# Attention kernel on one core: the x bank's work and the products with v move behind the second group's pair of each step

## The chip, the cores and the metric

The kernel runs on one core of a Trainium2 chip. The metric is the device time of one execution in microseconds (us), as the median of several runs. TensorE (PE) does the matmuls, VectorE (DVE) and ScalarE (ACT) read their results, GpSimd (POOL) works in on-chip memory alone, and SyncE (SP) issues the transfers.

## What is computed

Four layers stand one behind the other, on x of shape (16, 1024, 256), each added to its input: a state-space layer, a gated feed-forward layer, causal attention, and the same feed-forward layer again. The change touches only the attention:

```
x_proj = x @ Wqkv + bqkv                 # x is the normalised input; 16 heads of 16
att = jnp.einsum('bhtd,bhsd->bhts', q, k) * (1.0 / jnp.sqrt(jnp.float32(hd)))
att = jnp.where(causal, att, jnp.float32(-jnp.inf))
att = jax.nn.softmax(att, axis=-1)
y = att @ v
return y.transpose(0, 2, 1, 3).reshape(B, T, C) @ Wproj + bproj
```

## The kernel before

The attention goes over 16 batches b, and in each over 4 quads q of four heads. A quad has 20 steps, and a step has two groups g, 0 and 1, that lie on different halves of TensorE's rows. For each step and group TensorE issues a pair: a piece of the second pass of this quad (`second_piece`, line 1657: scores of keys against queries, less the row maximum, for the exponential), and beside it a piece of the first pass of a later quad for the other group (`first_piece`, line 1633: scores whose row maxima are wanted). Steps 14 and 15 have no first pass. In what follows "pair 8.1" is that of step 8 and group 1. Where a piece touches the diagonal, two small matmuls (`masked`, line 1603) add the mask.

Each pass has three banks of PSUM that are used in turn, so a pair can only start when the reader of the pair three before it is done: `second_wait` waits for the exponential of that pair (ScalarE, line 1525, counted by `exp_done`), and `first_wait` for its maxima (VectorE, line 1427, counted by `s1_free`). Only at the start of a batch is the turn of the second pass's banks begun anew: pair 0.0 of q = 0 waits for the exponential of the pair directly before it.

Two further kinds of work stand on TensorE's queue between the pairs.

- Every odd step has a product with v (`times_v`, line 1685), of the unit of two steps whose probabilities were finished two steps ago.
- In `x_events` is written which work uses the single bank `x_ps`, and at which step: "heads" (turning the finished heads, line 1717), "turn" and "out" (the output projection of the batch before, lines 1724 and 1732), and "project" 0 to 7 for later half batches (0 and 1 transposes, line 1699; 2 to 5 parts of q and k, line 1703; 6 and 7 v, line 1709). An event at `at` is issued in step `at + 1`, so at even steps. Eight of the ten even steps have one; steps 18 and 0 have none. `x_free` hands the bank back.

The readers' queues are laid down by step: in step s ScalarE does both exponentials and then what step s has for the x bank; VectorE does the maxima of group 1's and then of group 0's first-pass piece (that is, of pair s.0 and of pair s.1), and then what step s has for the x bank (lines 1412 to 1455). Behind that, in step 6 of q = 0 and q = 2, stands the preparation of a later half batch (`prepare`, lines 1398 to 1406), which there are 15 and 14 of in the loop. The orders of VectorE, ScalarE, GpSimd and SyncE are the same in both kernels; every queue runs in its own order.

Of the kernel before, what the change touches and what calls it, by code (L numbers as in the profile page):

```python
# [991 lines left out]
def attention_phase(nc, sem, identf, identb, x2, x3, wqkv, bqkv, wproj, bproj, qk_scratch, v_scratch):  # L992
# [36 lines left out]
    def x_events(q, first, more, more2):  # L1029

        heads = [] if first and q == 0 else [(1, "heads", 0), (7 if q == 1 else 5, "heads", 1)]
        finish = [] if first else {0: [(9, "turn", 0), (11, "out", 0), (13, "turn", 1), (15, "out", 1)],
                                   1: [(3, "turn", 2), (5, "turn", 3), (9, "out", 2), (11, "out", 3)]}.get(q, [])
        project = {0: [(3, 6), (7, 7)], 1: [(13, 0), (15, 1)], 2: [(3, 2), (7, 3), (9, 4), (11, 5), (13, 6), (15, 7)],
                   3: [(3, 0), (7, 1), (9, 2), (11, 3), (13, 4), (15, 5)]}[q] if (more2 if q == 3 else more) else []
        return sorted(heads + finish + [(s, "project", j) for s, j in project])

    def flags(b):
        if isinstance(b, int):
            return b == 0, b + 1 < NB, b + 2 < NB  # L1040
        return False, True, True
# [4 lines left out]
    def x_base(b, q):  # L1046

        before = X_PROLOGUE + sum(x_count(i) for i in range(b)) if isinstance(b, int) else \
            x_count(None) * b + (X_PROLOGUE + x_count(0) - x_count(None))
        return before + sum(len(x_events(i, *flags(b))) for i in range(q))  # L1050

    def projected(b, q):

        return ((2 * b + 2, 0), (2 * b + 3, 1), (2 * b + 3, 1), (2 * b + 4, 0))[q]

    def first_pass_at(q, step, more):

        if step < UNITS1 - LEAD:
            return (1, step + LEAD) if more or q < 3 else None
        if step >= STEPS - LEAD:  # L1060
            return (2, step - (STEPS - LEAD)) if more or q < 2 else None
        return None

    with ExitStack() as ctx:
# [83 lines left out]
        with nc.Block() as block:  # L1148
# [440 lines left out]
            def _(pe):  # L1589
# [27 lines left out]
                def first_wait(quad, unit, g):  # L1617
                    if g == 1 and unit == 0:
                        for side in range(2):
                            pe.wait_ge(laid_out[side], quad + 1)  # L1620
                    use = 2 * unit + 1 - g
                    if not isinstance(quad, int) or quad > 0 or use >= 3:
                        pe.wait_ge(s1_free, 2 * UNITS1 * quad + use - 2)

                def first_piece(buf, unit, g, k):

                    p, pieces = unit // len(PASS1), PASS1[unit % len(PASS1)]
                    if k >= len(pieces):
                        return
                    bank = s1_ps[(2 * unit + 1 - g) % 3]  # L1630
                    blk, t0, t1 = pieces[k]
                    col, w = sum(HD * (u1 - u0) for _, u0, u1 in pieces[:k]), HD * (t1 - t0)
                    last = mm(bank[:, col:col + w], rows_of(qs[buf], g, KROWS, p, BT * blk, BT * (blk + 1)),  # L1633
                              rows_of(ks[buf], g, KROWS, p, t0, t1), start=k == 0,
                              stop=k == len(pieces) - 1 and not diagonals(pieces, True))
                    if k == len(pieces) - 1:
                        if diagonals(pieces, True):
                            last = masked(bank[:, :], 0, g, diagonals(pieces, True))
                        last.then_inc(s1_full, 1)

                def second_wait(quad, q, step, g, first):
                    use = s2_use(q, step, g)
                    if use >= 3 or not first:
                        before = 3 if use >= 3 else (1, 4, 4)[use]
                        pe.wait_ge(exp_done, 2 * STEPS * quad + 2 * step + g - before + 1)
                    if step < 2 and g == 0:
                        pe.wait_ge(max_moved[step % 2], 128 * (quad + 1))

                def second_piece(buf, step, g, k):

                    u, p = step // 2, step % 2
                    if k >= len(PASS2[u]):
                        return
                    j, t0, t1 = PASS2[u][k]
                    bank = s2_ps[s2_use(buf, step, g) % 3]
                    col, w = sum(HD * (u1 - u0) for _, u0, u1 in PASS2[u][:k]), HD * (t1 - t0)
                    last = mm(bank[:, col:col + w], rows_of(ks[buf], g, SHIFT + 1, p, BT * j, BT * (j + 1)),  # L1657
                              rows_of(qs[buf], g, SHIFT + 1, p, t0, t1), start=k == 0,
                              stop=k == len(PASS2[u]) - 1 and not diagonals(PASS2[u], False))
                    if k == len(PASS2[u]) - 1:  # L1660
                        if diagonals(PASS2[u], False):
                            last = masked(bank[:, :], 1, g, diagonals(PASS2[u], False))
                        last.then_inc(s2_full, 1)
# [49 lines left out]
                def turn_heads(quad, e, index):  # L1713
                    pe.wait_ge(o_free, 2 * quad + e + 1)
                    pe.wait_ge(x_free, index)
                    for n in range(4):
                        last = pe.transpose(x_ps[:, n * P:(n + 1) * P], o_sb[:, e, n * P:(n + 1) * P], identf[:, :])
                    last.then_inc(x_full, 1)

                def turn_y(r, index):  # L1720
                    pe.wait_ge(x_free, index)
                    for f in range(KT):
                        for t in range(2):
                            last = pe.transpose(x_ps[:, (2 * f + t) * P:(2 * f + t + 1) * P], y_sb[:, f, 2 * r + t, :],
                                                identf[:, :])
                    last.then_inc(x_full, 1)
# [9 lines left out]
                def slot(b, q):  # L1736
                    first, more, more2 = flags(b)
                    quad, old = 4 * b + q, not first or q > 0
                    events = x_events(q, first, more, more2)
                    for step in range(STEPS):  # L1740
                        unit = first_pass_at(q, step, more)
                        for g in range(2):
                            second_wait(quad, q, step, g, first)
                            if unit is not None:
                                first_wait(quad + unit[0], unit[1], 1 - g)
                            for k in range(2):
                                second_piece(q, step, g, k)
                                if unit is not None:
                                    first_piece((q + unit[0]) % 4, unit[1], 1 - g, k)
                            for n, (at, kind, which) in enumerate(events):  # L1750
                                if g == 0 and at == step - 1:
                                    index = x_base(b, q) + n
                                    if kind == "project":
                                        project(*projected(b, q), which, index)
                                    elif kind == "heads":
                                        turn_heads(quad - 1, which, index)
                                    elif kind == "turn":
                                        turn_y(which, index)
                                    else:
                                        out(which, index)  # L1760
                            if g == 0 and step % 2 and (step >= 3 or old):
                                u = (step - 3) // 2
                                if u >= 0:
                                    times_v(quad, q, b, u, old)
                                else:
                                    times_v(quad - 1, (q - 1) % 4, b if q else b - 1, UNITS2 - 1, True)
                def sequence(b):
                    for q in range(4):
                        slot(b, q)
# [68 lines left out]
```

## Time and profile before

| what | value |
|---|---|
| median of 3 runs | 4366.06 us (4352.54 to 4367.1) |
| the profiled execution | 4354.76 us, its span 4352.9 us |
| mean granted TensorE clock | 0.975 |
| attention's loop | about 1240 to 3610 us of the span |

The profile is of one execution. Busy times are those of the engines' own records, and a matmul's end is modelled, so that a wait shows in the start of the next instruction rather than in the busy share. A group's idle time is that directly before it, with the engine that ended it.

### The profile page before, as it was taken

To read this page: it belongs to the slowest core of one execution; us is meant where nothing else is said; L and a number is where in the kernel's file an instruction comes from. 1 tells how busy PE (TensorE), PEld (TensorE's weight loads), DVE (VectorE), ACT (ScalarE), POOL (GpSimd) and SP (SyncE) were. 2 spreads that over 40 slices of the span, in tenths; PEclk is the share of its full clock that TensorE was granted. 3 is DMA by queue.
4 is the path that set the end of the run, shared out by engine and by line. 5 is a ranking of instruction groups with operands and counts; after the bars stand their busy time and mean duration, and the time that the engine had idled before them with its cause. 6 is when DMAs were issued, how large, how long until landed. Compare 5 with 4: busy or idle time off the path is not lost. (4 is left out here: it accounts for less than half of the span.)

```text
span 4352.9 us, 84136 instructions
## 1 busy us (share of the span) xinstructions
PE 4007.2 (92%) x29070; PEld 2585.5 (59%) x29070; DVE 3226.2 (74%) x8384; ACT 2253.3 (52%) x4326; POOL 1323.3 (30%) x1208
## 2 busy tenths in 40 slices
PE   5997999999489999999999999999999996999998
PEld 4886666666245555555555555555555554666665
DVE  6997677767367777777777777777777763777776
ACT  0100555555136666666666666666666663555544
POOL 2332113212432434343333324343433310221121
PEclk9998999999779999999999999999999998999999
DMA  1333111221577676676767677676767632123111
GB/s 55 101 101 117 63 58 58 78 96 39 96 115 106 105 105 109 105 109 101 117 101 111 105 111 105 102 121 102 108 94 115 87 45 78 59 70 104 58 58 58
DMA packets 735203, 394.28 MB, mean 91 GB/s; under 512 B 306096, under 2 KB 701872, under 8 KB 734896
## 3 DMA queue, kind: packets, MB, share of 16 engines
q1 hardware_dynamic: 734896, 390.21, 48.1%
q8 instruction: 190, 3.11, 0.4%
q14 instruction: 117, 0.96, 0.1%
HBM read 238.04 MB, written 150.99 MB: 89 GB/s over the span
## 5 line engine op out<-in xcount | busy, mean ns | idle before, releaser
L1427 DVE TENSOR_REDUCE att_maxima<-att_s 128x1 f32<-128x512 f32 (+3 forms) x3072 | 1521.1, 548 | 407.0 <-PE att_s L1603 214.8
L1525 ACT ACTIVATE att_probs<-att_s 128x512 f32<-128x512 f32 (+1 forms) x2560 | 1330.4, 557 | 880.2 <-PE att_s L1603 507.6
L1657 PE MATMUL att_s<-att_qs,att_ks 49*128 49x512 f32 (+3 forms) x3072 | 1000.6, 401 | 70.5 <-DVE att_maxima L1427 42.0
L1633 PE MATMUL att_s<-att_ks,att_qs 48*128 48x512 f32 (+3 forms) x3072 | 996.4, 409 | 2.0 <-DVE att_maxima L1427 1.6
L1657 PEld LDWEIGHTS att_s<-att_qs,att_ks 49*128 49x128 f32 x3072 | 474.1, 186 | 629.2 <-ACT att_probs L1525 410.3
L1685 PE MATMUL att_o_ps<-att_probs,att_vs 128*32 128x512 f32 (+3 forms) x6144 | 633.6, 499 | 1.4 <-issue 1.0
L1603 PE MATMUL att_s<-att_mask,att_places 64*128 64x64 bf16 (+1 forms) x5632 | 591.2, 209 | 0.5 <-issue 0.5
L1633 PEld LDWEIGHTS att_s<-att_ks,att_qs 48*128 48x128 f32 x3072 | 505.5, 188 | 17.0 <-DVE att_maxima L1427 8.6
L839 ACT ACTIVATE ffn_h<-ffn_h1p,ffn_b 128x512 f32<-128x512 f32 x384 | 243.2, 684 | 394.2 <-PE ffn_h1p L944 394.2
L749 DVE TENSOR_TENSOR ffn_zT_lo<-ffn_turned,ffn_zT_hi 128x1024 fp32r<-128x1024 f32 x192 | 234.2, 1220 | 253.5 <-ACT ffn_zT_hi L831 145.6
L926 PE MATMUL ffn_h2p<-ffn_h,ffn_w 128*128 128x512 f32 x768 | 366.2, 599 | 3.2 <-ACT ffn_h L839 1.8
L937 PE MATMUL ffn_h1p<-ffn_zT_hi,ffn_w_hi 128*128 128x512 f32 x768 | 344.1, 448 | 8.9 <-ACT ffn_zT_hi L829 8.9
L1603 PEld LDWEIGHTS att_s<-att_mask,att_places 64*128 64x128 bf16 x5632 | 284.0, 96 | 111.9 <-issue 43.6
L1344 POOL TENSOR_TENSOR att_x_res<-att_x_res,att_bp_row 128x512 f32<-128x512 f32 x64 | 81.3, 1283 | 752.0 <-DMA att_x_res<-x 751.6
L937 PE MATMUL ffn_h1p<-ffn_zT_hi,ffn_w_lo 128*128 128x512 f32 x768 | 304.4, 396 | 0.0
L916 PEld LDWEIGHTS ffn_turned<-identf,ffn_z 128*128 128x128 f32 x1536 | 169.8, 142 | 171.1 <-issue 76.7
L916 PE MATMUL ffn_turned<-identf,ffn_z 128*128 128x128 f32 x1536 | 211.4, 281 | 62.2 <-DVE ffn_z L721 34.4
L653 POOL TENSOR_TENSOR ffn_residual<-ffn_residual,ffn_z 128x768 f32<-128x768 f32 x64 | 177.0, 2765 | 276.2 <-DVE ffn_z L721 276.2
L640 POOL TENSOR_TENSOR ffn_var_eps<-ffn_moments,ffn_eps 128x4 f32<-128x4 f32 x64 | 12.8, 201 | 799.2 <-DVE ffn_moments L685 799.2
L1332 POOL CAST att_ks<-att_staged 113x1024 fp32r<-113x1024 f32 x128 | 251.6, 1989 | 0.0
L1332 POOL CAST att_qs<-att_staged 113x1024 fp32r<-113x1024 f32 x128 | 251.3, 1986 | 0.0
L1703 PE MATMUL att_x_ps<-att_xnT,att_wqkv 128*128 128x512 f32 x768 | 218.7, 421 | 25.0 <-DVE att_carrier L1418 20.0
(218 smaller groups left out, 6082.3 us busy)
## 6 DMA issues: line engine op xcount, KB each, us to landing
att_staged<-qk_scratch SPq DMA_DIRECT2D x768, 128.0 KB, 7.1
qk_scratch<-att_parts SPq DMA_DIRECT2D x128, 512.0 KB, 3.2
ffn_x<-x SPq DMA_DIRECT2D x64, 512.0 KB, 7.1
ffn_residual<-x SPq DMA_DIRECT2D x64, 512.0 KB, 4.9
ssm_x<-in_L_attn_a_x_dram SPq DMA_DIRECT2D x32, 512.0 KB, 3.8
x<-ssm_y SPq DMA_DIRECT2D x32, 512.0 KB, 2.9
x<-ffn_y SPq DMA_DIRECT2D x32, 512.0 KB, 5.0
att_x<-x SPq DMA_DIRECT2D x32, 512.0 KB, 13.2
```

The source lines that it names most:

```text
L749: v.tensor_tensor(zT_lo[k][:, :, :], turned_ps[:, :, :], zT_hi[k][:, :, :], ALU.subtract).then_inc(zT_lo_ready, 1)
L839: last = a(h1[k][:, f, :], h1_ps[:, f, :], ACT.Gelu, bias=b1[:, f:f + 1])
L916: last = pe.transpose(turned_ps[:, f, t * P:(t + 1) * P], z[c][cycle][:, t, f * P:(f + 1) * P], identf[:, :])
L926: last = mm(h2_ps[:, :], w2[:, f, :], h1[k][:, f, :], start=(f == 0), stop=(f == KT - 1))
L937: mm(h1_ps[:, o, :], part[:, f, cols], zT_hi[k][:, f, :], start=(f == 0 and i == 0), stop=False)
L1332: last = g.tensor_copy(stack[0:ROWS, :].rearrange("p (t c) -> p t c", c=HD)[:, e * n:(e + 1) * n, :], staged[side][0:ROWS, :, e * n:(e + 1 ...
L1427: last = v.tensor_reduce(maxima_of[p][:, g, blk, 1 if t0 else 0:2 if t0 else 1], s1_ps[(2 * unit + 1 - g) % 3][:, col:col + w], AX.X, ALU.max)
L1525: a(probs[u % 2][2 * g + p][:, 0:n], bank[:, 0:n], ACT.Exp).then_inc(exp_done, 1)
L1603: last = mm(blocks[:, at, GROUP * half:GROUP * (half + 1)], places[rows, 2 * (1 - k) + half, :], mask[rows, 1 - k, 0:len(cols), :], start= ...
L1633: last = mm(bank[:, col:col + w], rows_of(qs[buf], g, KROWS, p, BT * blk, BT * (blk + 1)), rows_of(ks[buf], g, KROWS, p, t0, t1), start=k ...
L1657: last = mm(bank[:, col:col + w], rows_of(ks[buf], g, SHIFT + 1, p, BT * j, BT * (j + 1)), rows_of(qs[buf], g, SHIFT + 1, p, t0, t1), star ...
L1685: last = mm(o_ps[32 * i:32 * i + 32, HD * (t0 - first_t):HD * (t1 - first_t)], vs[s][:, NBLK * head + j, :], probs[u % 2][i][:, col:col + ...
```

## The change

In the loop of a step, the x bank's event and the product with v are issued behind the pair of group 1, where they stood between the pairs of group 0 and group 1. Nothing is added and nothing is taken away; the masks are issued as before.

```
                             for n, (at, kind, which) in enumerate(events):
-                                if g == 0 and at == step - 1:
+                                if g == 1 and at == step - 1:
                                     index = x_base(b, q) + n
...
-                            if g == 0 and step % 2 and (step >= 3 or old):
+                            if g == 1 and step % 2 and (step >= 3 or old):
                                 u = (step - 3) // 2
                                 if u >= 0:
                                     times_v(quad, q, b, u, old)
```

TensorE's queue in steps 8 and 9 of q = 2 of the first batch: pair 8.0, then what follows it. Before:

```order
L1657 MATMUL att_s_0<-att_qs,att_ks 128x512 [waits att_s1_free,att_exp_done]
L1633 MATMUL att_s_0<-att_ks,att_qs 128x384
L1633 MATMUL att_s_0<-att_ks,att_qs 128x128
L1603 MATMUL att_s_0<-att_mask,att_places 128x2x64 x2
L1703 MATMUL att_x_ps<-att_xnT,att_wqkv 128x512 [waits att_x_free]
L1703 MATMUL att_x_ps<-att_xnT,att_wqkv 128x512 x5
L1657 MATMUL att_s_1<-att_qs,att_ks 128x512 [waits att_s1_free,att_exp_done]
```

and with the change:

```order
L1657 MATMUL att_s_0<-att_qs,att_ks 128x512 [waits att_s1_free,att_exp_done]
L1633 MATMUL att_s_0<-att_ks,att_qs 128x384
L1633 MATMUL att_s_0<-att_ks,att_qs 128x128
L1603 MATMUL att_s_0<-att_mask,att_places 128x2x64 x2
L1657 MATMUL att_s_1<-att_qs,att_ks 128x512 [waits att_s1_free,att_exp_done]
L1633 MATMUL att_s_1<-att_ks,att_qs 128x384
L1633 MATMUL att_s_1<-att_ks,att_qs 128x128
L1603 MATMUL att_s_1<-att_mask,att_places 128x2x64 x2
L1703 MATMUL att_x_ps<-att_xnT,att_wqkv 128x512 [waits att_x_free]
```

The six matmuls of line 1703 stood ahead of pair 8.1 and its two waits; now they stand behind it.

The end of the same quad on TensorE, steps 16 and 17, from the first row of the v projection (line 1709). Before:

```order
L1709 MATMUL att_x_ps<-att_wqkv,att_xnT 128x256 [waits att_x_free]
L1709 MATMUL att_x_ps<-att_wqkv,att_xnT 128x256 x11
L1657 MATMUL att_s_2<-att_qs,att_ks 128x384 [waits att_s1_free,att_exp_done]
L1633 MATMUL att_s_1<-att_ks,att_qs 128x512
L1657 MATMUL att_s_2<-att_qs,att_ks 128x128
L1603 MATMUL att_s_2<-att_mask,att_places 128x2x64 x2
L1657 MATMUL att_s_0<-att_qs,att_ks 128x384 [waits att_s1_free,att_exp_done]
```

and with the change, from the row before it:

```order
L1603 MATMUL att_s_2<-att_mask,att_places 128x2x64 x2
L1709 MATMUL att_x_ps<-att_wqkv,att_xnT 128x256 [waits att_x_free]
L1709 MATMUL att_x_ps<-att_wqkv,att_xnT 128x256 x11
L1657 MATMUL att_s_0<-att_qs,att_ks 128x384 [waits att_s1_free,att_exp_done]
```

Pair 16.1 (the one that writes `att_s_2`) has gone ahead of the projection, and pair 17.0 follows it directly.

## Rows read from the trace of the kernel before

In the windows the columns are start and end, length, busy us (and instructions) of PE, its weight loads, DVE, ACT and POOL, then TensorE's granted clock as a share of full speed, the busy share of the DMA engines, and GB/s. A timeline gives the start, the length and the instruction; in brackets stands the idle time before it and what ended it.

**Rows 1.** Windows: the attention's loop, columns in the sentence above.

```profile
1240.00:3610.00 2370.00, 2282.99 (x20754) 1378.13 (x20753) 1821.08 (x4169) 1497.76 (x2982) 828.38 (x691) 0.99 0.68 102
```

**Rows 2.** The page's groups: the maxima, and the pairs' leading matmul.

```profile
L1427 DVE TENSOR_REDUCE att_maxima<-att_s 128x1 f32<-128x512 f32 (+3 forms) x3072 | 1521.1, 548 | 407.0 <-PE att_s L1603 214.8
...
L1657 PE MATMUL att_s<-att_qs,att_ks 49*128 49x512 f32 (+3 forms) x3072 | 1000.6, 401 | 70.5 <-DVE att_maxima L1427 42.0
```

**Rows 3.** Timeline of PE, a quad q = 0, steps 6 to 8.

```profile
2156.91 0.65 PE L1717 MATMUL att_x_ps<-identf,att_o 128*128 128x128 f32 x4
2157.50 0.50 PE L1657 MATMUL att_s<-att_qs,att_ks 49*128 49x512 f32 x1
...
2159.67 1.70 PE L1709 MATMUL att_x_ps<-att_wqkv,att_xnT 128*128 128x256 f32 x12
2161.98 0.47 PE L1657 MATMUL att_s<-att_qs,att_ks 49*128 49x512 f32 x1 [0.61 <-DVE att_maxima L1427]
```

**Rows 4.** Timeline of DVE in the same steps.

```profile
2158.11 0.69 DVE L1427 TENSOR_REDUCE att_maxima<-att_s 128x1 f32<-128x512 f32 x1 [0.15 <-PE att_s L1603]
2158.72 0.25 DVE L1444 RECIPROCAL att_recip<-att_x_ps 128x16 f32<-128x16 f32 x1
...
2159.34 1.40 DVE L1398 BATCH_NORM_STATS2 att_stats<-att_x 128x6 f32<-128x256 f32 x4
...
2161.18 1.72 DVE L1427 TENSOR_REDUCE att_maxima<-att_s 128x1 f32<-128x512 f32 x3
```

**Rows 5.** Timeline of PE, a quad q = 2, step 8: pair 8.1.

```profile
2234.49 0.46 PE L1657 MATMUL att_s<-att_qs,att_ks 49*128 49x512 f32 x1 [0.78 <-DVE att_maxima L1427]
```

**Rows 6.** Timeline, a quad q = 3, steps 16 to 18: PE, then ACT and DVE.

```profile
2138.17 1.64 PE L1703 MATMUL att_x_ps<-att_xnT,att_wqkv 128*128 128x512 f32 x6 [0.34 <-DVE att_carrier L1418]
2139.74 0.44 PE L1657 MATMUL att_s<-att_qs,att_ks 49*128 49x384 f32 x1
...
2143.23 0.35 PE L1657 MATMUL att_s<-att_qs,att_ks 49*128 49x256 f32 x1 [0.66 <-ACT att_probs L1525]
...
2140.89 0.68 ACT L1535 ACTIVATE att_parts<-att_x_ps,att_b_qk 128x512 fp32r<-128x512 f32 x1
...
2141.61 0.75 DVE L1415 SCALAR_TENSOR_TENSOR att_parts<-att_x_ps,att_b_qk,att_parts 128x512 fp32r<-128x512 f32 x1 [0.65 <-ACT att_parts L1535]
2142.40 0.69 DVE L1427 TENSOR_REDUCE att_maxima<-att_s 128x1 f32<-128x512 f32 x1
```

**Rows 7.** Timeline of PE at the start of a batch: pair 19.1, then pair 0.0.

```profile
2145.40 0.38 PE L1657 MATMUL att_s<-att_qs,att_ks 49*128 49x256 f32 x1
...
2146.33 0.50 PE L1657 MATMUL att_s<-att_qs,att_ks 49*128 49x512 f32 x1 [0.29 <-ACT att_probs L1525]
```

**Rows 8.** Windows (columns as in rows 1): idle gaps of PE, and stretches behind them.

```profile
1705.30:1706.60 1.30, 0.04 (x1) 0.00 (x0) 0.77 (x2) 0.31 (x1) 0.00 (x0) 1.00 1.25 121
1708.00:1718.50 10.50, 10.50 (x53) 6.60 (x53) 7.09 (x22) 4.95 (x10) 9.00 (x10) 0.51 0.91 124
2083.70:2084.80 1.10, 0.00 (x0) 0.02 (x1) 1.10 (x7) 0.00 (x0) 0.55 (x2) 1.00 1.74 120
2087.00:2090.50 3.50, 3.50 (x13) 2.58 (x13) 2.22 (x6) 1.09 (x2) 3.50 (x3) 0.52 0.02 2
...
2009.30:2010.50 1.20, 0.00 (x0) 0.00 (x0) 1.08 (x5) 1.20 (x3) 0.00 (x0) 1.00 1.46 173
2012.00:2024.00 12.00, 12.00 (x96) 6.82 (x99) 8.97 (x21) 7.55 (x15) 11.84 (x13) 1.00 0.49 86
```

**Rows 9.** Windows, from a quad's first product with v to the next quad's.

```profile
1698.83:1741.14 42.31, 40.48 (x339) 25.18 (x337) 28.49 (x68) 22.99 (x47) 19.21 (x17) 0.88 0.76 104
2072.72:2113.63 40.91, 39.13 (x338) 24.18 (x337) 30.03 (x74) 24.43 (x49) 16.95 (x15) 0.96 0.76 124
2150.72:2187.88 37.16, 36.00 (x338) 22.55 (x336) 28.34 (x68) 22.99 (x47) 19.32 (x17) 1.00 0.82 118
2222.75:2261.81 39.06, 37.69 (x338) 23.14 (x337) 30.03 (x74) 24.43 (x49) 16.96 (x15) 1.00 0.78 130
```

More of the change, by code:

```diff
@@ L1750, in slot @@
                             for n, (at, kind, which) in enumerate(events):
-                                if g == 0 and at == step - 1:
+                                if g == 1 and at == step - 1:
                                     index = x_base(b, q) + n
@@ L1760, in slot @@
                                         out(which, index)
-                            if g == 0 and step % 2 and (step >= 3 or old):
+                            if g == 1 and step % 2 and (step >= 3 or old):
                                 u = (step - 3) // 2
```

## The prediction

> **What bounds the kernel now.** I first read the windows by stage. The change touches only the attention, whose loop is 2370 us; TensorE is busy in 96% of it at a clock of 0.99, VectorE in 77% and ScalarE in 63% [rows 1]; VectorE's largest part is the maxima, 1521 us [rows 2]. So TensorE's queue sets the time, and the total of its work does not change: the same matmuls are issued, and between two fillers (x work or a product with v) there are still two pairs. What can change is the time in which TensorE stands at a wait. The groups of the page say how little of that is seen: 70.5 us in all before the pairs' leading matmul [rows 2]. So I went to the timelines, to find where in a quad the waits are, what ends each, and where it stands once the fillers have moved by one pair. The waits recur in the same steps of nearly every batch, so one quad of each kind is enough. There are four kinds of place.
>
> **Step 8 of q = 0 and q = 2: a longer wait.** VectorE is late here. Behind the maxima of step 6 it divides the heads, then prepares a half batch (statistics alone 1.40 us), and only at 2161.18 begins the maxima of step 7 [rows 4]. Pair 8.1 needs the first of them. It starts at 2161.98, after 0.61 us of idle TensorE [rows 3]; for q = 2 the same wait is 0.78 us [rows 5]. Before the change the projection of step 8 lies ahead of this wait and covers it: it starts at 2159.67 and lasts 1.6 us until the next thing could start. With the change it stands behind pair 8.1 and cannot pass it. Pair 8.1 comes to its wait at 2159.7, since otherwise the same pairs and fillers lie ahead. When is it released? VectorE's chain starts from pair 6.1, which now goes ahead of the 0.59 us of heads (2156.91 instead of 2157.50), and the heads are read as soon as the maxima are through; these ran without a pause but for 0.15 us. That brings the division from 2158.72 to about 2158.35, and the release from 2161.98 to 2161.6. The wait is then 1.9 us in place of 0.7. For q = 2 it is 0.8 + 1.6 - 0.3 = 2.1. Then the projection of 1.6 us must still be done, while the pairs behind it find their banks free. Per place I count the projection's 1.6 less the earlier release, less the 0.2 that pair 9.0 no longer waits for the second maxima: **+1.0 us**, so +2.0 per batch.
>
> **Ends of q = 1 and q = 3: shorter waits.** In q = 3 the part projected in step 16 waits 0.34 for the bank, then pair 16.1 runs, and what it brings (exponential, maxima) stands ahead of the readers of the projection. ScalarE copies it only at 2140.89, VectorE takes it at 2141.61 and reaches the maxima of step 17 at 2142.40, and pair 18.1 waits for them until 2143.23 [rows 6]. With the change pair 16.1 runs in the 0.34 that was waited, its readers are done during the projection, ScalarE can copy at 2140.0, and the first maxima of step 17 end at about 2142.2. The pair reaches its wait at 2142.15. VectorE is then still short of breath at steps 18 and 19: 0.69 for a maximum against some 0.43 for a pair, so about 0.5 us of small waits stay. I take -0.65 for q = 3 and, where the projection is a short transpose, -0.5 for q = 1: **-1.15 per batch**.
>
> **Seams of quads.** At a batch's start pair 0.0 follows pair 19.1 by 0.93 us, where 0.43 is the pair itself, because it waits for the exponential directly before it [rows 7]. Now 1.0 us of product with v lies between. That gives back 0.5, of which VectorE, still behind at step 1, takes 0.2 again; the other three seams gain under 0.1 each: **-0.5 per batch**.
>
> **Other steps with a projection of q and k.** These go the wrong way a little. From the end of the projection VectorE's first maxima of the next step come 0.15 + 0.6 (ScalarE) + 0.8 + 0.65 us later, plus 0.1 for the signal (the durations of rows 6), so after 2.3 to 2.4; TensorE needs that bank after two pairs, 1.0 us of product and one pair, so after 2.2. I count 0.1 to 0.3 for each such place, 1.75 per batch in seven places, against 1.1 of waits at these steps now: **+0.65**.
>
> **The sum without the clock** is 2.0 - 1.15 - 0.5 + 0.65 = +1.0 us per batch, +15 us over the 15 batches that have all of it. I give it a range of -5 to +35.
>
> **The clock.** A wait of 1.9 us is longer than any in this part of the loop now, and I looked at what the shorter ones do. The granted clock is 1.00 nearly throughout, yet after a gap of 1.30 us it was 0.51 for 10.5 us; after one of 1.10 (the wait at step 8 itself, in one batch longer than its usual 0.78) it was 0.52 for 3.5 us. A gap of 1.20 did not lower it [rows 8]. That is the change between 2.4 and 1.2 GHz. None of the usual waits of 0.6 to 0.8 did so. What a fall costs is read from whole quads: of q = 0, 42.31 us with it against 37.16 without, less the gap of 1.30: 3.9. For q = 2, 40.91 against 39.06, less the 0.35 by which its gap was longer: 1.5 [rows 9]. With the change 15 gaps of 1.8 and 14 of 2.1 us stand where none stood. If every one lowers the clock, that is 15 x 3.9 + 14 x 1.5 = 79 us. As a gap can fall so that nothing happens, I take 85%: +67.
>
> The Trainium skill, "TensorE: Matmul & The Clock Gate", section on HAM oscillation, ties the loss of the clock to idle gaps between bursts that are longer than any counted here, and by it the 67 us would not come. The trace does not agree: the clock fell after 1.10 us. The same page (Part 3, "The mechanism") has matmuls start and end strictly in program order, and the trace agrees: nothing of TensorE's starts in the 0.61 us before pair 8.1.
>
> **Forecast.** 15 + 67 = +82 us. On the profiled execution's 4354.76 that is 4437; the median of the runs stands 11 us above it, so **4446 us**, 1.8% slower. Some 0.5% (22 us) is what a measurement tells from no change.
>
> **Rivals.**
> - *The clock holds.* Then only +15 us are left: 4381, range 4361 to 4401. For it speaks the gap of 1.20 us that lowered nothing; against it that the longest did, and that the gaps to come are longer still. It is what the page above would have.
> - *Faster: VectorE is not late at step 8.* In the changed order maxima and x work are taken up sooner all along the quad. If that frees VectorE by 1.6 us instead of 0.4 before the preparation, step 8 costs nothing and no gap arises; with the steps in between also at nothing, -1.65 per batch are left, -25 us: 4341. It decides when pair 8.1 is released before about 1.0 us after it comes to its wait. Against it: VectorE was idle for only 0.15 us ahead of that chain, so it can't have been held up by more.
> - *Nothing in effect*: the small terms and step 8 cancel and the clock holds: 4366.
> - *Worse*: every gap lowers the clock for the longest time seen, in q = 2 too: 29 x 3.9 + 35 = 148 us, 4514.
>
> **How the numbers follow.** The forecast's case (clock falls at most places) has 0.66, with 4400 to 4480 as its own range; the clock holds 0.18, of which a quarter is above +22 us; nothing 0.06; faster 0.07; worse 0.03. The range from 4370 to 4482 leaves out the faster case, the lower part of the clock's holding and the worst. Slower by over 0.5%: 0.66 + 0.03 + 0.05 = 0.74; within: 0.19; faster: 0.07.
>
> **What would show it.** In the changed profile the groups of line 1657 should have idle time before them of 70 + 29 x 1.2, some 100 us, with VectorE's maxima as releaser; at step 8 of q = 0 and 2 the wait should be 1.8 to 2.1 us, followed in most by a clock near 0.5; attention's mean clock should fall from 0.99 to about 0.95. Pair 18.1 of q = 3 should wait under 0.3 us, and pair 0.0 at a batch's start not at all. The stages outside the attention should stay as they are. I am wrong if pair 8.1 waits under a microsecond, or if the clock stays at 1.00 behind it.

## The result and the profile after

| | before | changed |
|---|---|---|
| median of 20 runs | 4352.81 us | 4377.68 us |
| lowest run | 4336.71 us | 4354.28 us |
| span of the profiled execution | 4352.9 us | 4380.4 us |
| mean granted TensorE clock | 0.975 | 0.963 |

The changed kernel takes 1.0056 times as long (95% interval 1.0039 to 1.0073), so it is slower by some 24 us. Forecast were 82. The sign is right, the size is not. (The kernel before had a median of 4366.06 us in the three runs that the forecast started from, and has 4352.81 us in twenty; one of these twenty took 5260.1 us and does not count in the ratio.)

The page of the changed kernel, its groups for the maxima and for the pairs' leading matmul:

```profile
L1427 DVE TENSOR_REDUCE att_maxima<-att_s 128x1 f32<-128x512 f32 (+3 forms) x3072 | 1493.3, 549 | 282.1 <-PE att_s L1633 177.5
...
L1657 PE MATMUL att_s<-att_qs,att_ks 49*128 49x512 f32 (+3 forms) x3072 | 1012.6, 402 | 100.4 <-DVE att_maxima L1427 82.0
```

The idle time before the pairs rose from 70.5 us [rows 2] to 100.4, with VectorE's maxima as releaser; that is the forecast's "some 100". The windows of the changed kernel show where the time is (columns as in rows 1): first a stage outside the attention, then its loop, then the wait at step 8 and what follows it in one batch, then the same in another. In the first window the kernel before has the same busy time, 890.32 us.

```profile
0.00:1000.00 1000.00, 890.24 (x4506) 658.07 (x4507) 773.70 (x2185) 330.70 (x593) 249.27 (x255) 0.98 0.24 79
1240.00:3630.00 2390.00, 2282.03 (x20747) 1369.78 (x20746) 1803.51 (x4164) 1503.05 (x2982) 828.19 (x691) 0.97 0.67 101
1877.70:1879.50 1.80, 0.01 (x2) 0.04 (x2) 1.68 (x9) 0.72 (x2) 0.58 (x1) 1.00 1.30 245
1881.00:1885.00 4.00, 4.00 (x21) 1.46 (x20) 1.55 (x4) 1.68 (x3) 3.84 (x6) 0.57 1.25 172
2184.20:2186.10 1.90, 0.16 (x4) 0.00 (x0) 1.78 (x10) 0.88 (x2) 0.00 (x0) 1.00 1.16 246
2186.10:2193.00 6.90, 6.85 (x55) 3.97 (x55) 5.45 (x13) 4.65 (x9) 6.46 (x8) 1.00 1.20 146
```

The loop is some 20 us longer, with the same PE work in it as in rows 1 and a clock of 0.97 instead of 0.99. From the first product with v to the last it takes 2344 us before and 2367 changed, and the stages ahead of it and behind it differ by 4 us at most, so the loss is in the loop. The same gap of 1.80 us is followed by a clock of 0.57 in the first batch and of 1.00 in the second.

The timeline of the changed kernel, PE in steps 6 to 8 of a quad q = 0, against rows 3:

```profile
2181.89 0.66 PE L1717 MATMUL att_x_ps<-identf,att_o 128*128 128x128 f32 x4
...
2183.72 0.50 PE L1657 MATMUL att_s<-att_qs,att_ks 49*128 49x512 f32 x1
...
2186.15 0.47 PE L1657 MATMUL att_s<-att_qs,att_ks 49*128 49x512 f32 x1 [1.80 <-DVE att_maxima L1427]
2186.71 0.50 PE L1709 MATMUL att_x_ps<-att_wqkv,att_xnT 128*128 128x256 f32 x2
```

and DVE in the same steps, against rows 4:

```profile
2181.69 1.29 DVE L1427 TENSOR_REDUCE att_maxima<-att_s 128x1 f32<-128x512 f32 x2 [0.48 <-PE att_s L1603]
2182.90 0.25 DVE L1444 RECIPROCAL att_recip<-att_x_ps 128x16 f32<-128x16 f32 x1
...
2183.52 1.40 DVE L1398 BATCH_NORM_STATS2 att_stats<-att_x 128x6 f32<-128x256 f32 x4
...
2185.35 1.25 DVE L1427 TENSOR_REDUCE att_maxima<-att_s 128x1 f32<-128x512 f32 x2
```

Pair 8.0 starts at 2183.72, pair 8.1 would follow at 2184.35 and is held until 2186.15: the statistics of the preparation stand ahead of the maxima that it needs, and the projection (2186.71), which hid 1.6 us of this, now comes behind. All 29 places show such a wait: mostly 1.80 us in q = 0 and 1.86 in q = 2, once 1.50 and once 1.57, and in a few disturbed batches up to 3.05.

Whole quads of the changed kernel: two of q = 0, with and without a fall of the clock behind step 8, and two of q = 2, without and with one.

```profile
1869.19:1908.12 38.93, 36.67 (x340) 22.49 (x336) 28.16 (x68) 22.90 (x47) 19.26 (x17) 0.96 0.83 124
2175.87:2213.25 37.38, 35.12 (x340) 22.15 (x337) 28.19 (x68) 22.83 (x47) 19.28 (x17) 1.00 0.85 118
...
2994.40:3034.45 40.05, 37.29 (x340) 22.67 (x336) 29.78 (x74) 24.72 (x49) 16.94 (x15) 1.00 0.84 132
2549.37:2590.69 41.32, 38.73 (x341) 23.65 (x337) 29.77 (x74) 24.73 (x49) 16.92 (x15) 0.96 0.74 123
```

Between the quads shown a fall costs 1.55 us in q = 0 and 1.27 in q = 2. These are the usual ones; over thirteen whole batches in the middle of the loop, the eight quads q = 0 with a fall take 1.5 to 2.95 us more than those without (mean 2.1), and the ten quads q = 2 take 1.0 to 2.4 us more (mean 1.6). Of the 29 places 21 have a fall (read from the granted clock in windows of half a microsecond), and most falls last some 3.5 us. Counted in the same way, TensorE stands at its lower clock for 118 us between 1275 and 3440 us, against 31.5 before.

Beside the forecast places I measured every stretch from the start of one filler (work of the x bank or a product with v) to the start of the next, and added up the median of each over the batches, leaving out those at a low clock. Such a typical batch takes 146.9 us, before 148.2. Without the clock the change is a gain. By place, per batch: step 8 +2.22 us; the ends of q = 1 and 3 -1.28; the four seams -0.92; all the rest -1.3.

The ends are as forecast. Here is the timeline of the changed kernel, q = 3 from step 16 into the next batch, against rows 6 and 7; the L1657 rows at 2167.51 and 2168.03 are pairs 18.0 and 18.1, the one at 2170.79 is pair 0.0:

```profile
2163.99 1.66 PE L1703 MATMUL att_x_ps<-att_xnT,att_wqkv 128*128 128x512 f32 x6
...
2166.51 1.06 PE L1685 MATMUL att_o_ps<-att_probs,att_vs 128*32 128x512 f32 x8
2167.51 0.38 PE L1657 MATMUL att_s<-att_qs,att_ks 49*128 49x256 f32 x1
2168.03 0.35 PE L1657 MATMUL att_s<-att_qs,att_ks 49*128 49x256 f32 x1
...
2169.79 1.07 PE L1685 MATMUL att_o_ps<-att_probs,att_vs 128*32 128x384 f32 x16
2170.79 0.49 PE L1657 MATMUL att_s<-att_qs,att_ks 49*128 49x512 f32 x1
...
```

Neither the projection nor pair 18.1 nor pair 0.0 has a wait listed; 0.66 and 0.29 us stood before the last two. At the seam, however, the wait that is gone was worth little: before the change the four pairs from 19.1 to 1.0 took 2.14 us from the start of the first to the next filler in every seam, with that wait or without; the four that stand there now, 0.0 to 1.1, take 2.05 us in every seam.

### The profile page after: what moved, and what is told of

It is laid out like the page before. It is cut to its first block and busy times, and to the rows that moved or that the text cites. A ratio compares the mean times of both kernels' runs of the same rounds, so it can differ in the third digit from the quotient of the medians.

```text
span 4380.4 us, 84136 instructions
## 1 busy us (share of the span) xinstructions
PE 4016.5 (92%) x29070; PEld 2583.7 (59%) x29070; DVE 3210.7 (73%) x8384; ACT 2258.7 (52%) x4326; POOL 1323.2 (30%) x1208
## 5 line engine op out<-in xcount | busy, mean ns | idle before, releaser
L1427 DVE TENSOR_REDUCE att_maxima<-att_s 128x1 f32<-128x512 f32 (+3 forms) x3072 | 1493.3, 549 | 282.1 <-PE att_s L1633 177.5
L1525 ACT ACTIVATE att_probs<-att_s 128x512 f32<-128x512 f32 (+1 forms) x2560 | 1296.4, 556 | 677.9 <-PE att_s L1603 354.1
L1657 PE MATMUL att_s<-att_qs,att_ks 49*128 49x512 f32 (+3 forms) x3072 | 1012.6, 402 | 100.4 <-DVE att_maxima L1427 82.0
L1657 PEld LDWEIGHTS att_s<-att_qs,att_ks 49*128 49x128 f32 x3072 | 481.7, 188 | 672.8 <-ACT att_probs L1525 466.3
L1603 PE MATMUL att_s<-att_mask,att_places 64*128 64x64 bf16 (+1 forms) x5632 | 581.4, 209 | 2.6 <-issue 2.5
L1703 PE MATMUL att_x_ps<-att_xnT,att_wqkv 128*128 128x512 f32 x768 | 232.7, 442 | 19.3 <-DVE att_carrier L1418 15.1
```

The source lines that it names most:

```text
L1427: last = v.tensor_reduce(maxima_of[p][:, g, blk, 1 if t0 else 0:2 if t0 else 1], s1_ps[(2 * unit + 1 - g) % 3][:, col:col + w], AX.X, ALU.max)
L1525: a(probs[u % 2][2 * g + p][:, 0:n], bank[:, 0:n], ACT.Exp).then_inc(exp_done, 1)
L1603: last = mm(blocks[:, at, GROUP * half:GROUP * (half + 1)], places[rows, 2 * (1 - k) + half, :], mask[rows, 1 - k, 0:len(cols), :], start= ...
```

## The experiments

Ratios are to the kernel before, with 95% intervals; 0.01 is 43.5 us. "Low" is the time at the lower clock between 1275 and 3440 us of the profiled execution, of which there is one for each kernel; "clock" is the mean granted clock over all runs of a kernel.

| kernel | median us | ratio | low, us | clock |
|---|---|---|---|---|
| before | 4352.81 | 1 | 31.5 | 0.972 |
| changed | 4377.68 | 1.0056 (1.0039 to 1.0073) | 118 | 0.960 |
| e1_step8_back | 4301.87 | 0.9882 (0.9851 to 0.9914) | 7 | 0.972 |
| e2_step8_alone | 4460.1 | 1.0229 (1.0197 to 1.026) | 164 | 0.959 |
| e8_wait_filled | 4338.54 | 0.9965 (0.9947 to 0.9982) | 40.5 | 0.973 |
| e3_prepare_14 | 4300.42 | 0.9864 (0.9832 to 0.9897) | 34.5 | 0.971 |
| e4_before_prepare_14 | 4332.99 | 0.9968 (0.995 to 0.9986) | 7 | 0.969 |
| e5_x_alone | 4430.46 | 1.0191 (1.0168 to 1.0214) | 146 | 0.960 |
| e6_v_alone | 4387.85 | 1.0084 (1.0065 to 1.0104) | 55 | 0.966 |
| e9_parts_between | 4343.54 | 0.9981 (0.996 to 1.0003) | 119.5 | 0.961 |
| e7b_before_no_mask | 4244.43 | 0.9746 (0.9709 to 0.9784) | 153.5 | 0.956 |
| e7a_after_no_mask | 4262.91 | 0.978 (0.9756 to 0.9805) | 132 | 0.955 |

### Step 8 put back, and step 8 alone

e1 is the changed kernel with the step-8 event of q = 0 and 2 between the pairs again:

```
-                                if g == 1 and at == step - 1:
+                                if g == (0 if step == 8 and q in (0, 2) else 1) and at == step - 1:
```

> The changed kernel, but the projection of step 8 of q = 0 and q = 2 stands between pairs 8.0 and 8.1 again. Theory A (the change gains outside step 8, and loses at step 8 by an uncovered wait of 1.8 us and the clock that falls behind it): idle time before pair 8.1 back to 0.6 to 0.8 us, no clock near 0.5 behind it, and a time about 50 us under the kernel before (ratio about 0.988). Rival B (the order gains nothing outside step 8; the loss was smaller than forecast because gap and clock cost little): within 10 us of the kernel before, 0.998 to 1.002.

e2 is the kernel before with that one event behind its pair 8.1:

```
-                                if g == 0 and at == step - 1:
+                                if g == (1 if step == 8 and q in (0, 2) else 0) and at == step - 1:
```

> The kernel before, with one thing of the change alone: the projection of step 8 of q = 0 and q = 2 behind pair 8.1. Theory A: the whole loss without any of the gain: 2.2 us per batch for the wait (32 us in all) and about 24 falls of the clock at 1.3 to 1.5 us (34 us): +66 us, ratio 1.015. Rival B: only as much as the whole change, +24 us, 1.0056 or less.

e1 is faster than both kernels, 0.9882: two events in each batch turn a loss of 0.6% into a gain of 1.2%. The wait before pair 8.1 is shorter than was expected, 0.17 us in q = 0 and 0.27 in q = 2. Pair 8.1 of e1 in its timeline, q = 2:

```profile
2206.81 1.66 PE L1703 MATMUL att_x_ps<-att_xnT,att_wqkv 128*128 128x512 f32 x6
2208.73 0.47 PE L1657 MATMUL att_s<-att_qs,att_ks 49*128 49x512 f32 x1 [0.27 <-DVE att_maxima L1427]
```

e2 has the loss alone, +2.3%, more than was expected of it. Pair 8.1 of q = 0 in its timeline:

```profile
2213.63 0.59 PE L1657 MATMUL att_s<-att_qs,att_ks 49*128 49x512 f32 x1 [2.24 <-DVE att_maxima L1427]
2214.45 2.92 PE L1709 MATMUL att_x_ps<-att_wqkv,att_xnT 128*128 128x256 f32 x12
```

The wait is 2.2 us instead of 1.8, since in this kernel nothing ahead of VectorE's chain has moved up, and the projection behind it takes 2.92 us instead of 1.70: the clock is down. Windows of e2, the wait and the stretch behind it:

```profile
2211.40:2213.60 2.20, 0.00 (x0) 0.00 (x0) 2.08 (x11) 1.25 (x3) 1.21 (x1) 1.00 1.49 171
2213.50:2217.50 4.00, 3.87 (x19) 3.37 (x19) 1.91 (x5) 0.69 (x2) 3.84 (x6) 0.57 1.19 97
```

In e2 the clock falls within or behind all 26 waits of 1.94 to 2.71 us at this place.

### The wait filled

e8 is the changed kernel, and the matmuls of the step-8 projection are issued once more ahead of pair 8.1, their result unread. VectorE's lateness stays, only TensorE is busy in it.

```
+                            for n, (at, kind, which) in enumerate(events):
+                                if g == 1 and step == 8 and at == 7 and q in (0, 2) and kind == "project":
+                                    project(*projected(b, q), which, x_base(b, q) + n, False)
```

> The changed kernel, with the matmuls of the projection of step 8 (q = 0 and q = 2) issued once more ahead of pair 8.1, into the same bank, with nobody told; the real ones follow as in the changed kernel. TensorE then works 1.6 of the 1.8 us that it stood idle. Theory A: the clock stays at 1.00 there, and the time is the changed kernel's less what the clock took, 30 to 40 us less: ratio to the kernel before 0.997. Rival B (a low clock behind the gap costs nothing, because VectorE and ScalarE set the pace then): the same as the changed kernel, 1.005 to 1.006.

Timeline of e8 at step 8 of a quad q = 0, and the window behind pair 8.1:

```profile
1863.17 1.70 PE L1709 MATMUL att_x_ps<-att_wqkv,att_xnT 128*128 128x256 f32 x12
1865.04 0.47 PE L1657 MATMUL att_s<-att_qs,att_ks 49*128 49x512 f32 x1 [0.17 <-DVE att_maxima L1427]
1865.60 1.70 PE L1709 MATMUL att_x_ps<-att_wqkv,att_xnT 128*128 128x256 f32 x12
```

```profile
1865.50:1872.00 6.50, 6.50 (x56) 3.55 (x52) 5.04 (x12) 4.76 (x9) 5.32 (x7) 1.00 1.12 134
```

Pair 8.1 starts 2.44 us after pair 8.0 here and 2.43 us after it in the changed kernel, so the copy fills the wait and does not lengthen it, and the clock stays at 1.00. Extra work makes the kernel faster: e8 stands 0.0091 (some 40 us) below the changed kernel. That is the clock's part. In the two profiled executions the time at the lower clock differs by 77.5 us, which would make 0.5 us for each; but over all runs the mean clock is 0.9729 against 0.9596, which is some 118 us of low clock, so a third of a microsecond for each is the better figure. From e8 to e1 it is 0.0083, 36 us, or 1.2 us in each of 29 places: the wait itself.

### The preparation moved away

e3 is the changed kernel, e4 the kernel before, both with the preparation at step 14:

```
-    LAY_OUT_AT, PREPARE_AT, PIECES = 10, 6, 2
+    LAY_OUT_AT, PREPARE_AT, PIECES = 10, 14, 2
```

> The changed kernel, with the preparation of a half batch behind step 14 on VectorE instead of step 6 (GpSimd's part in step 16). Theory A: steps 14 and 15 have no maxima, so VectorE has the 1.8 us to spare there; the wait at 8.1 is under 0.5 us as in q = 3, the clock holds, and the time is about 75 us under the kernel before (0.983). Rival C: VectorE comes late to the maxima of steps 16 and 17 instead, and pairs 17.1 to 18.1 of q = 0 and 2 wait about a microsecond more: 0.990 or above.

> The kernel before with the preparation behind step 14 in place of step 6. Its waits at step 8 are 0.7 and 0.8 us and those of pair 9.0 0.2, so 1.9 us per batch are to be had: 25 us under the kernel before, 0.994. Rival: the wait moves to steps 16 to 18, 0.998 or above. Against the changed kernel with the same edit (0.9864) it tells what the order itself is worth when step 8 is out of play: theory A says 0.008 to 0.01 of the time.

With VectorE on time, nothing is left of the loss: e3 has 0.9864, which the intervals don't tell from e1. e4 is 0.9968, so with a step 8 that waits little in either order the changed order is worth -0.0104, some 45 us, known to about 16 by the intervals. The typical batch at full clock says the same: 143.2 us in e3 and 146.3 in e4, -3.1, or -46 us over 15. (e4 was expected at 0.994. Its batch is 1.8 us shorter than the 148.2 of the kernel before, as worked out, but its mean clock is a little lower, 0.969 against 0.973 in the runs beside it.) The page's L1657 group of e3:

```profile
L1657 PE MATMUL att_s<-att_qs,att_ks 49*128 49x512 f32 (+3 forms) x3072 | 1006.2, 401 | 49.5 <-DVE att_maxima L1427 28.4
```

and that of e4:

```profile
L1657 PE MATMUL att_s<-att_qs,att_ks 49*128 49x512 f32 (+3 forms) x3072 | 996.5, 400 | 53.2 <-DVE att_maxima L1427 24.8
```

The listed waits differ by 3.7 us only. These two profiled executions are 17.6 us apart, not 45 (their spans are 4298.6 and 4316.2 us), and that of e3 has 27.5 us more of low clock; even so most of the difference is in no listed wait: the pairs themselves follow each other more closely.

### One kind of work moved at a time

e5 moves only the x bank's events behind the second pair, e6 only the products with v:

```
-                                if g == 0 and at == step - 1:
+                                if g == 1 and at == step - 1:
```

```
-                            if g == 0 and step % 2 and (step >= 3 or old):
+                            if g == 1 and step % 2 and (step >= 3 or old):
```

> The kernel before, with the x bank's work behind the second pair and the products with v left between the pairs. Theory A (pairs of one step side by side are cheaper; step 8 loses by wait and clock): only the even steps have their pairs side by side, so half of the 50 us of gain, and all of the loss at step 8: some 50 us over the kernel before, 1.008 to 1.015. Rival B (the gain is in the x work's readers, who no longer stand behind the second pair's): as the whole change or better, 1.006 or less.

> The kernel before, with the products with v behind the second pair and the x bank's work left between the pairs. Theory A: the odd steps have their pairs side by side, half of the gain, and the projection of step 8 still covers VectorE's delay, so no long gap and no low clock: 15 to 30 us under the kernel before, 0.993 to 0.997. Rival B (gain in the x work's readers): 0.998 to 1.005, since x work has not moved.

e5 has the step-8 loss (waits mostly of 1.85 to 2.07 us, and 24 stretches at the lower clock between 1275 and 3440 us, against 4 before), and came out above its range. e6 was expected faster or equal, and is slower by 0.8%: both theories missed. Neither half of the change is good by itself: +1.9% and +0.8%, together +0.6%. With one kind moved, blocks of one and of three pairs alternate between the fillers, in place of two and two. The typical batch of e6 takes 149.3 us at full clock, 1.1 more than before, of which 0.5 lie at step 8 of q = 0 and 2 and 0.4 at the ends of q = 1 and 3; over 15 batches that is 17 of its 37 us. Its timeline behind the projection of step 8, where pairs 8.1, 9.0 and 9.1 now stand together:

```profile
2178.20 0.47 PE L1657 MATMUL att_s<-att_qs,att_ks 49*128 49x512 f32 x1 [0.60 <-DVE att_maxima L1427]
...
2179.46 0.46 PE L1657 MATMUL att_s<-att_qs,att_ks 49*128 49x512 f32 x1 [0.16 <-DVE att_maxima L1427]
```

The first waits 0.60 and the third 0.16 us. Over the whole kernel, though, the listed waits before pairs are not longer than before (67.7 us against 70.5). The other 20 us go with a lower clock (0.966 over all runs, against 0.973 in the runs beside it); what lowers it in e6 I did not settle.

### The projection's parts put back

The forecast has +0.65 us per batch for the steps in which a part of q or k (project 2 to 5) is projected. e9 is e3 with these between the pairs.

```
-                                if g == 1 and at == step - 1:
+                                late = 0 if kind == "project" and 2 <= which < 6 else 1
+                                if g == late and at == step - 1:
```

> The changed kernel with the preparation behind step 14, and in addition the projections of parts of q and k (events 2 to 5) between the pairs as before; they are followed by ScalarE, VectorE and a wait, and pairs 10.1 and 12.1 of q = 2 and q = 3 now wait about 0.5 us each behind them. Theory A: these waits (some 1.5 us per batch) go, but the pairs of these steps are no longer side by side (0.15 us each, 1.2 per batch): within 0.003 of the version without this edit (0.984 to 0.989). Rival B (side by side costs and gains nothing): 0.980 to 0.982.

It is 0.0117 above e3, a loss of some 51 us, where theory A allowed 0.003. The order alone does not make it. A whole batch of e9 without a fall, then one of e3:

```profile
2752.20:2895.86 143.66, 140.53 (x1314) 85.41 (x1312) 115.25 (x267) 93.87 (x189) 54.91 (x46) 1.00 0.73 112
```

```profile
2123.30:2266.56 143.26, 141.04 (x1315) 85.41 (x1313) 114.75 (x267) 94.66 (x189) 54.91 (x46) 1.00 0.73 112
```

That is 0.4 us per batch, 6 us in all, as theory A has it. The other 45 us lie in batches in which the clock falls: it is low for 119.5 us against 34.5, and 0.961 against 0.971 over all runs. Five of these falls stand behind the wait of pair 18.1 of q = 3, which the projection put back in step 16 makes 0.63 us long again. One of them, timeline and window:

```profile
2290.86 0.35 PE L1657 MATMUL att_s<-att_qs,att_ks 49*128 49x256 f32 x1 [0.63 <-DVE att_maxima L1427]
```

```profile
2293.30:2310.00 16.70, 16.70 (x116) 11.31 (x112) 9.33 (x22) 7.38 (x14) 0.00 (x0) 0.50 1.23 134
```

The other nine stand behind gaps of 1.2 to 3.5 us that recur at no fixed place; the kernel before has such gaps too, and why e9 has more of them than e3 is open.

### Without the masks

e7b is the kernel before and e7a the changed one, both without the mask matmuls: the diagonal blocks are left unmasked.

```
+                    return []
```

> The kernel before without the small mask matmuls of either pass, so that the blocks on the diagonal are not masked. It is the base for the next run. 5632 small matmuls of some 0.1 us between starts are gone, partly covered: 0.96 to 0.98 of the kernel before.

> The changed kernel without the mask matmuls, so that the blocks on the diagonal are not masked. Theory M (pairs side by side are cheaper because the masks of both groups stand together): without masks that gain is gone and the loss at step 8 stays, so it is slower than the kernel before without masks by about 1.2% (0.010 to 0.015). Rival W (the gain is shorter waits for ScalarE and VectorE, whatever the masks): slower than it by at most 0.6%, as with masks.

Between the two the ratio is 1.0035, and their intervals overlap, so the whole times did not move as the theory on the masks wanted (1.010 to 1.015); they lie where rival W has them. They don't decide, because e7b has trouble of its own, once in most batches. Its timeline and the window behind:

```profile
2536.21 0.35 PE L1658 MATMUL att_s<-att_qs,att_ks 49*128 49x256 f32 x1 [0.91 <-DVE att_maxima L1427]
```

```profile
2537.00:2551.00 14.00, 13.74 (x88) 7.83 (x90) 9.11 (x22) 6.24 (x14) 0.00 (x0) 0.63 1.23 136
```

Its batches take 142 to 145 us with such a fall. Two of thirteen have next to none, 139.2 us and this one:

```profile
1683.85:1822.59 138.74, 130.55 (x963) 70.23 (x961) 114.00 (x267) 94.36 (x189) 54.98 (x46) 1.00 0.75 115
```

What can be compared is a stretch nearly without waits and at full clock, q = 1 from the product with v of step 3 to that of step 17. The kernel before, then the changed one:

```profile
2187.88:2212.97 25.09, 25.01 (x218) 14.72 (x216) 19.47 (x44) 15.96 (x33) 10.64 (x8) 1.00 0.43 71
```

```profile
2213.25:2237.47 24.22, 24.22 (x217) 14.34 (x214) 18.95 (x42) 16.35 (x34) 10.58 (x8) 1.00 0.48 75
```

and without masks, before (e7b) and changed (e7a):

```profile
2148.45:2171.54 23.09, 22.84 (x164) 12.01 (x163) 19.03 (x44) 16.19 (x34) 10.63 (x8) 1.00 0.59 86
```

```profile
2152.79:2175.63 22.84, 22.84 (x165) 12.15 (x163) 19.04 (x43) 16.05 (x34) 10.60 (x8) 1.00 0.51 80
```

The order is worth 0.87 us with the masks and 0.25 without, and all of this 0.25 is a wait: PE is busy 22.84 in both. In this stretch, then, the gain is bound to the masks. The same holds of the batch as a whole, place by place at full clock (step 8 left out, since every batch of e7a has a fall there). The changed order moves the seams and all the rest by -2.2 us per batch with the masks and by nothing without them (-0.03); the ends of q = 1 and 3, whose gain is in waits, by -1.3 in both. In q = 0 and 1, where nothing else waits, the rest alone is -0.7 and -0.8 per batch with the masks, and -0.14 and 0.0 without. So of the 3.5 us per batch that the order is worth away from step 8, 2.2 hang on the masks and 1.3 on the waits at the ends.

## Why the prediction was right in sign and wrong in size

**The account.** In the typical batch at full clock the change is worth -1.3 us, -19 us over 15. The clock costs +40 by e8, whose clock is that of the kernel before. Sum: +21, measured +24. The forecast had +15 and +67. The experiments cut the first term in two: the order away from step 8 is worth -51 (e1; -45 by e3 against e4) and the wait +36. That -51, +36 and +40 add up to the measured change is no test, since each of these steps begins where the one before ends. The test is the trace, which at full clock has -3.5 us per batch away from step 8 (-52) and +2.2 at it (+33). Each is known to some 10 to 15 us only, by the intervals.

**Step 8, right.** The place, the cause, the length (1.80 and 1.86, forecast 1.9 and 2.1) and the price without the clock (+2.22 per batch, forecast +2.0) came as worked out, the length a little below. e1 and e2 show that it carries the whole loss, e3 that VectorE's preparation is what makes it.

**The ends, right; the seams, right in sign by another cause.** The ends gave -1.28 per batch against -1.15. The seams gave -0.92 against -0.5, but not where the forecast had it. It took 0.3 of the 0.5 from the wait of pair 0.0 at a batch's start and under 0.1 from each other seam; measured are some 0.23 in each of the four, the batch's start no more than the others, and without the masks hardly anything (-0.14 in all four). The wait at a batch's start cost nothing, because the pairs behind it came the closer; the gain is that of the next paragraph.

**First failed step: "the total of its work does not change".** The matmuls are the same, but they don't cost the same in either order. Away from the places named, the forecast has +0.65 us per batch, the measurement -1.3; with the 0.4 by which the seams gave more that is some 35 us in the run, which is the whole miss of the sum without the clock (+15 forecast, -19 measured). The waits that the forecast worked out did come (in q = 2 and 3 the block behind a projection of q or k is 1.25 to 1.40 us long instead of 0.8 to 0.9), and cost more than it had: these two quads stand at +0.2 and +0.05 where q = 0 and 1, which have none of them, stand at -0.7 and -0.8. But in every quad the pairs themselves are some 0.75 us cheaper, a term that the forecast put at nothing. The two timelines of PE show how. Before, q = 1, pairs 9.1 and 10.0, later 10.1 and 11.0:

```profile
2048.22 0.50 PE L1657 MATMUL att_s<-att_qs,att_ks 49*128 49x512 f32 x1
...
2049.01 1.99 PE L1732 MATMUL att_x_ps<-att_wproj,att_yT 128*128 128x256 f32 x8
2050.93 0.49 PE L1657 MATMUL att_s<-att_qs,att_ks 49*128 49x512 f32 x1
...
2051.79 0.64 PE L1685 MATMUL att_o_ps<-att_probs,att_vs 128*32 128x512 f32 x4
```

Changed, pairs 10.0 and 10.1, which have masks, then 11.0 and 11.1, which have none:

```profile
2068.67 0.50 PE L1657 MATMUL att_s<-att_qs,att_ks 49*128 49x512 f32 x1
...
2069.58 1.99 PE L1732 MATMUL att_x_ps<-att_wproj,att_yT 128*128 128x256 f32 x8
2071.51 0.50 PE L1657 MATMUL att_s<-att_qs,att_ks 49*128 49x512 f32 x1
...
2072.18 1.06 PE L1685 MATMUL att_o_ps<-att_probs,att_vs 128*32 128x512 f32 x8
```

Before, from step 7 to step 11 every block of two pairs holds one with masks and one without: 0.79 and 0.86 us. Changed, the kinds stand together: 0.91 and 0.67, 0.07 less for the two blocks. At steps 14 and 15, of the second pass alone, it is 0.90 + 0.52 before and 0.51 + 0.67 now. That this gain vanishes without the masks is shown; why a pair is cheaper beside its like (the two groups lie on different halves of the rows, and their matmuls may overlap better) is only argued.

**Second failed step: what a fall of the clock costs.** The share of places was nearly right, 21 of 29 where 85% was forecast. The size was not: 3.9 us in q = 0 came from a single quad of before with a fall of 10.5 us [rows 8, 9], a rare one; behind step 8 most lasted some 3.5 us, and a fall cost 2.1 us in q = 0 on the mean, and 1.6 in q = 2, where 1.5 had been taken. The term was +67, measured +40. The kernel of e2, in which the waits are longer, shows more: 132.5 us more of low clock than before, and +100 us in all.

The Trainium skill ("TensorE: Matmul & The Clock Gate", section on HAM oscillation), whose rule on idle gaps would have had the clock hold here, is not borne out by this trace: a gap of 1.80 us was followed by 0.57.

**The rivals.** "The clock holds" gave 4381 us, near the 4377.68 measured, by luck: the clock did fall, and the number started from a time before that was 13 us too high (its +15 on 4352.81 would be 4368). "Faster: VectorE is not late" fell with the wait of 1.80 us; e3 shows what it would have been, and more than was worked out for it (4300 us, not 4341), by the cheaper pairs.

## What to carry to other kernels

When work is moved past a wait, ask first what that work hid: here two of the events moved in each batch carried the whole loss, and the same change with them left in place (0.9882) or with the late reader's other work elsewhere (0.9864) is the faster kernel. A count of equal instructions is no equal cost: measure the stretch between two fixed points in the old order, and see whether blocks of different make-up have different prices before calling the total unchanged. Price a rare event from several instances, not from the longest.

## What the runs showed of the hardware

- The granted clock fell from 1.00 to near 0.5 behind gaps of TensorE from 0.63 us (e9, five times) and 0.91 us (e7b) to 2.7 us (e2), but not behind each: in the changed kernel 21 of 29 waits at step 8, most of 1.80 to 1.87 us, were followed by a fall, and one of 1.80 (at 2184.35) was not; in e2 it fell at all 26 of 1.94 to 2.71 us. The equal waits of 0.66 us in the kernel before had none. Most falls in the changed kernel lasted some 3.5 us, those in e7b 10 to 17. Their price was about a third of a microsecond for each at the lower clock (e8 against the changed kernel, over all runs).
- Redundant matmuls in a wait made the kernel 0.9% faster (e8 against the changed kernel): the clock was low for 40.5 us instead of 118.
- Two neighbouring pairs cost 0.79 to 0.86 us with masks on one of them, and 0.91 or 0.67 with masks on both or on neither; without the mask matmuls the order made no difference to them.
